# The first cell's images: copied raw from the input into the cell's own rows and normalised there, in place of a normalised tile that is stored and loaded again

## The reference

```python
for col in range(4):
    for row in range(4):
        if col == 0: ins = [input_tensor] if row == 0 else [outs[row - 1][-1]]
        elif row == 0: ins = [outs[row][0], outs[row + 1][1]]
        elif row == 3: ins = [outs[row][0], outs[row - 1][-1]]
        else: ins = [outs[row][0], outs[row + 1][1], outs[row - 1][-1]]
        outs[row] = _cell(W[col, row], b[col, row], ins)   # conv 3x3, bias, relu, split into right/up/down
return outs[-1][0]
```

## Time and profile before

| | us |
|---|---|
| median of 3 runs (lowest, highest) | 1264.2 (1263.89, 1266.4) |
| profiled execution, its own time | 1268.22 |
| its span | 1266.4 |
| PE busy | 1184.0 (93%) |
| DVE, ACT, POOL busy | 767.2, 676.1, 385.3 |
| granted TensorE clock, mean | 0.984 |

### The profile page before, as it was taken

The page is one execution under the profiler, slowest core; times in us unless marked ns, Lnnn a source line. Parts: engine busy times, 40 slices in busy tenths (PEclk is TensorE's granted clock), DMA queues, the critical chain, the costliest instruction groups (busy, mean ns, idle before and its releaser), DMA issues.

```text
span 1266.4 us, 15022 instructions
## 1 busy us (share of the span) xinstructions
PE 1184.0 (93%) x5178; PEld 878.6 (69%) x5178; DVE 767.2 (61%) x967; ACT 676.1 (53%) x737; POOL 385.3 (30%) x552
## 2 busy tenths in 40 slices
PE   2889999999999999989999999999999997999995
PEld 2656677666666677766666677777777775777773
DVE  6898962455656522245664652226665789989952
ACT  2677754344454434445444443344444789789821
POOL 7322233334512012412113213633233542104212
PEclk9999999999999999989999999999999998999997
DMA  6799998999999967899999987988789424776773
GB/s 172 225 251 251 278 270 244 180 169 205 212 199 201 228 184 205 214 177 208 200 212 185 195 224 203 246 213 224 195 210 201 58 33 73 108 114 109 125 124 59
DMA packets 103183, 233.67 MB, mean 185 GB/s; under 512 B 35316, under 2 KB 48196, under 8 KB 94724
## 3 DMA queue, kind: packets, MB, share of 16 engines
q1 hardware_dynamic: 80608, 179.28, 64.9%
q0 software_dynamic: 16064, 24.70, 10.7%
q10 hardware_dynamic: 6436, 28.74, 7.3%
HBM read 123.59 MB, written 85.19 MB: 165 GB/s over the span
## 4 chain that ended last, share of the span: by engine, by line
PE 59%; SPq 14%; DVE 12%; issue 6%; DMA 5%; ACT 3%; POOL 1%; DVEq 0%; ACTq 0%; POOLq 0%
PE PB L1736 52%; SPq L808 11%; PE PB L1705 5%; DMA F<-F 2%; DVE S L1586 2%; DVE S L1573 2%; DVE S L1579 1%; DVE F L1566 1%; SPq L839 1%; DMA S<-lattice 1%; DMA lattice<-S 1%; ACT F L1144 1%; SPq L790 1%; PE PB L1696 1%; DVE F L1449 1%
## 5 line engine op out<-in xcount | busy, mean ns | idle before, releaser
L1736 PE MATMUL PB<-F,WA 128*96 128x512 f32 (+1 forms) x3792 | 916.4, 403 | 22.2 <-DVE F L1461 9.0
L1736 PEld LDWEIGHTS PB<-F,WA 128*96 128x96 f32 (+1 forms) x3792 | 661.1, 175 | 268.5 <-ACT F L1144 16.8
L1144 ACT ACTIVATE F<-S 128x2116 fp32r<-128x2116 f32 (+4 forms) x160 | 261.5, 1635 | 212.8 <-issue 75.4
L1155 ACT ACTIVATE S<-PB,BIAS 96x512 f32<-96x512 f32 (+1 forms) x320 | 212.5, 683 | 272.2 <-PE PB L1736 270.1
L1449 DVE TENSOR_TENSOR F<-S,F 128x1089 fp32r<-128x1089 f32 (+2 forms) x80 | 121.5, 1518 | 172.4 <-ACT F L1144 171.6
L1451 DVE TENSOR_TENSOR F<-S,F 128x1058 fp32r<-128x1058 f32 x64 | 80.7, 1261 | 187.5 <-ACT F L1144 186.8
L1461 DVE CAST F<-F 64x528 fp32r<-64x528 f32 (+4 forms) x304 | 184.6, 657 | 3.5
L906 POOL DMA_DIRECT2D WA<-taps x76 | 56.9, 750 | 356.7 <-ACT S L1155 304.2
L1705 PE MATMUL PB<-F,WA 128*128 128x512 f32 x576 | 144.5, 407 | 14.9 <-DVE F L1566 14.9
L1705 PEld LDWEIGHTS PB<-F,WA 128*128 128x128 f32 x576 | 110.2, 193 | 43.6 <-issue 16.0
L1452 DVE TENSOR_TENSOR F<-S,F 64x1058 fp32r<-64x1058 f32 x64 | 82.0, 1282 | 0.0
(11 more groups left out here) (131 smaller groups left out, 742.0 us busy)
## 6 DMA issues: line engine op xcount, KB each, us to landing
S<-lattice SPq DMA_DIRECT2D x448, 66.1 KB, 5.2
lattice<-S SPq DMA_DIRECT2D x32, 817.5 KB, 6.1
S<-lattice SPq DMA_DIRECT2D x158, 136.1 KB, 3.4
S<-lattice SPq DMA_DIRECT2D x72, 272.5 KB, 5.3
lattice<-S ACTq DMA_DIRECT2D x50, 272.5 KB, 4.7
lattice<-S ACTq DMA_DIRECT2D x16, 817.5 KB, 6.6
lattice<-S SPq DMA_DIRECT2D x48, 272.5 KB, 3.9
S<-lattice SPq DMA_DIRECT2D x158, 70.1 KB, 3.2
```

Source lines behind the costliest of these rows:

```text
L1144: act.activation(piece_view(s, h, 0), raw_view(s, h), ACT.Copy).then_inc(hi_ready, 1)
L1155: act.activation(wide(to[:, at:at + TS])[:, :, 0:RX], pixels(RING_BANK[n % SLOTS_O][0:cell.rows, :]), ACT.Relu, bias=BIAS[0:cell.rows, k:k ...
L1736: last = nc.tensor.matmul(bank, WA[0:rows, first:first + cell.rows], wide(FZ[0:rows, i % SLOTS_F, base:base + TS])[:, :, 0:RX], start=j == ...
```

## The change

The tile XN, its stores, the copies between tiles and the loads of cell 0 from HBM go. In their place SP loads each image of x raw, a second time, into partitions 64 to 127 of its own slot, in four DMAs: two sets of rows, each twice, for even and odd columns (`copy_loads`). Each moves 16 channels x 32 rows of 64 floats, 128 KB. ACT (`upper_rows`) and DVE (`image_rows`) read these with a stride of two columns and write the normalised image into partitions 0 to 63 of the same slot; a masked product and two memsets on DVE put back the zeros of the border. Scale and bias are now made for 128 partitions x 8 images, since an image's rows carry the image in the free index: PE's product on the statistics has 16 columns in place of 2.

Around it: three loads of constants become one; the table of ACT is loaded early; cell 0's tap stores and loads are halved between SP and POOL; the stores of cell 0's outputs move from ACT's queue to SP's; the raw taps of cell 2 and those of two later convolutions are loaded by SP behind all images; the memsets of the start are cut to borders and spread differently over DVE and POOL. Cells 1 to 15 and all that follows are the same.

```diff
@@ layout and DMAs of an image
+        def image_copy(b):
+            at = b % SLOTS_K * PIECE
+            return flat[COPY_ROWS:P, at:at + COPY_SIZE]
+        def copy_loads(b):
+            rows = image_copy(b)
+            for r in range(2):
+                src = x[b].rearrange("c (i r) w -> r c i w", r=2)[r]
+                for s in range(2):
+                    first = r * WD + s
+                    dst = rows[r * HALO + s:(r + 1) * HALO:2, first:first + HT // 2 * WD]
+                    yield dst.rearrange("c (i w) -> c i w", w=WD), src
@@ SP
-            sp.wait_ge(turned, TURN_AT["cell0"])
-            load_taps(2)
-            sp.wait_ge(xn_act, 1)
-            sp.wait_ge(xn_dve, 1)
+            def load_copy(b):
+                if b >= SLOTS_K:
+                    sp.wait_ge(image_ready, b - SLOTS_K + 1)
+                for dst, src in copy_loads(b):
+                    sp.dma_start(dst, src).then_inc(copy_loaded[b % SLOTS_K], 16)
+            sp.wait_ge(kr_clear, 1)
+            for b in range(3):
+                load_copy(b)
...
+            for dst, src in first_half(tap_stores("cell0")):
+                sp.dma_start(dst, src).then_inc(tp0_stored, 16)
+            load_copy(3)
...
+            for dst, src in first_half(cell_spread(cells[0])):
+                sp.dma_start(dst, src).then_inc(w0_loaded, 16)
+            for b in range(HALF, B):
+                load_copy(b)
+            load_taps(2)
...
-                if ACT_STORED <= s // B < NC - 1:
+                if s < B or ACT_STORED <= s // B < NC - 1:
@@ ACT
+            def upper_rows(b):
+                rows = slice(COPY_ROWS, P)
+                act.wait_ge(copy_loaded[b % SLOTS_K], dma_total(copy_loads(b)) * (b // SLOTS_K + 1))
+                if b >= SLOTS_K:
+                    act.wait_ge(raw_read, copied_before[b - SLOTS_K + 1])
+                last = normalise(image_part(b, False), copy_part(b, False), b, rows)
+                if b % 2:
+                    last = normalise(image_part(b, True), copy_part(b, True), b, rows)
+                last.then_inc(upper_ready, 1)
...
-            for r, s, h in XN_ORDER[0::2]:
-                last = normalise(xn_rows(r, s, h), channel_rows(r, s, h), 0)
-            last.then_inc(xn_act, 1)
...
-            for i in range(2):
-                for dst, src in input_stores(i):
-                    act.dma_start(dst, src).then_inc(input_stored[i], 16)
+            upper_rows(0)
+            split_hi(0, 0)
+            upper_rows(1)
+            split_hi(1, 0)
+            upper_rows(2)
             turned_hi_part("cell1")
...
+                if s + 3 < B:
+                    upper_rows(s + 3)
@@ DVE
+            def image_rows(b):
+                rows = slice(COPY_ROWS, P)
+                if b % 2 == 0:
...
+                    nc.vector.tensor_scalar(image_part(b, True), copy_part(b, True), RS[rows, b:b + 1],
+                                            NBI[rows, b:b + 1], ALU.mult, ALU.add).then_inc(dve_step, 1)
...
+                dve.wait_ge(upper_ready, b + 1)
+                raw = raw_slot(b)
+                ends = wide(raw[0:COPY_ROWS, 0:PATCH])[:, :, 0:RW:RW - 1]
+                nc.vector.tensor_tensor(ends, ends, MASK[:, :].rearrange("p (q m) -> p q m", q=1)
+                                        .broadcast_to([COPY_ROWS, PATCH // RW, 2]), ALU.mult).then_inc(dve_step, 1)
...
+                nc.vector.memset(raw[0:HALO, TS:EVEN], 0.0)
+                nc.vector.memset(raw[HALO:COPY_ROWS, 0:RW], 0.0).then_inc(image_ready, 1)
```

More of the change, by code:

```diff
@@ L435, in piece_view, with copy_part, image_part @@
             return to.rearrange("p (t f) -> p t f", t=4) if cell.kind == "33" else to
[L437 to L444, removed]
+        def image_copy(b):
[9 more added lines that the diff above has]
+                    yield dst.rearrange("c (i w) -> c i w", w=WD), src
+        def copy_part(b, lower):
+            rows = image_copy(b)
+            if lower:
+                return rows[:, WD:WD + RQ * 2 * WD].rearrange("p (q f) -> p q f", f=2 * WD)[:, :, 0:WD + 1:2]
+            return rows.rearrange("p (q f) -> p q f", f=2 * WD)[:, :, 0:WD + 1:2]
+        def image_part(b, lower):
+            raw = raw_slot(b)[0:COPY_ROWS]
+            return wide(raw[:, EVEN:PATCH] if lower else raw[:, 0:EVEN])
         def row_halves(b, s):
             return OT[:, b % 2].rearrange("p y (w s) -> p s y w", s=2)[:, s]
-        XN_ORDER = [(r, s, h) for r in range(2) for s in range(2) for h in range(2)]
         def staged(s):
@@ L516, in output_stores @@
                 yield from image_store(k, b, st)
[L518 to L532, removed]
         def image_store(p, b, st):
@@ L794, in _ @@
                 q, before = halves_before[s] % SLOTS_K, last_user[s]
[L795 to L801, removed]
-                    for i in range(2):
-                        sp.wait_ge(input_stored[i], 2 * 16)
-                        sp.wait_ge(image_loaded[i], loads_after[i])
                 if k:
+                    if COPIES[cells[before // B].kind]:
+                        sp.wait_ge(raw_read, copied_before[before + 1])
+                    else:
+                        sp.wait_ge(lo_ready, pieces_before[before + 1])
                     sp.wait_ge(image_stored[b], 16 * stores_before[k])
-                for dst, src in direct_loads(s) if s < INPUT_PARTS[0] else input_loads(s):
-                    sp.dma_start(dst, src).then_inc(image_loaded[q], 16)
+                    for dst, src in input_loads(s):
+                        sp.dma_start(dst, src).then_inc(image_loaded[q], 16)
                 if s >= STORE_LAG:
@@ L856, in _ @@
             pool.memset(NHALF[:, :], -0.5).then_inc(pool_const, 1)
-            pool.memset(flat[:, 0:2 * PIECE], 0.0).then_inc(kr_clear, 1)
-            pool.memset(ST[:, :, :], 0.0).then_inc(st_clear, 1)
+            pool.memset(W3[:, :, :, :].bitcast(F32), 0.0).then_inc(wa_clear, 1)
+            for start in (0, SEG + 1):
+                pool.memset(ST[:, :, start:start + 1], 0.0)
+                pool.memset(ST[:, :, start + RW:start + LEAD:RW], 0.0)
+                pool.memset(ST[:, :, start + LEAD:start + TOP], 0.0)
+                pool.memset(ST[:, :, start + HOFF + RW:start + SEG:RW], 0.0)
+            last = pool.memset(ST[:, :, SEG:SEG + 1], 0.0)
+            last.then_inc(st_clear, 1)
+            pool.memset(FZ[:, :, 2 * PIECE:FSLOT].bitcast(F32), 0.0).then_inc(wa_clear, 1)
             pool.wait_ge(pool_const, 1)
@@ L990, in spread_kan @@
                     pool.dma_start(dst, src).then_inc(w2_loaded, 16)
-            store_taps("cell0")
-            norm(slice(1, 2), slice(0, 1), 1)
+            pool.wait_ge(turned_hi, TURN_AT["cell0"])
+            pool.wait_ge(turned_lo, TURN_AT["cell0"])
+            for dst, src in second_half(tap_stores("cell0")):
+                pool.dma_start(dst, src).then_inc(tp_stored, 16)
+            norm(slice(0, B), slice(0, B), 1)
+            pool.wait_ge(tp0_stored, dma_total(first_half(tap_stores("cell0"))))
+            pool.wait_ge(tp_stored, tp_after["cell0"])
+            for dst, src in second_half(cell_spread(cells[0])):
+                pool.dma_start(dst, src).then_inc(w0_spread, 16)
             clear_taps("cell1")
-            for dst, src in cell_spread(cells[0]):
-                pool.dma_start(dst, src).then_inc(w0_loaded, 16)
             store_taps("cell1")
@@ L1116, in _ @@
             act.dma_start(OB_IN[1:2, :], l3bias.rearrange("(a c) -> a c", a=1)).then_inc(bias_loaded, 16)
+            act.wait_ge(pool_const, 1)
+            act.activation(VE[:, 0:1], TWOS[:, :], ACT.Copy)
             def turned_hi_part(name):
@@ L1394, in _ @@
             dve.wait_ge(dve_step, next(steps))
[L1395 to L1402, removed]
-            dve.wait_ge(bias_loaded, 3 * 16)
-            for yi in range(YI):
-                nc.vector.tensor_copy(BN_REP[:, yi], BN_IN[:, :])
-                last = nc.vector.tensor_copy(OB_REP[:, yi], OB_IN[:, :])
@@ L1408, in _ @@
-            last.then_inc(bias_rep, 1)
-            turned_lo_part("cell1")
-            clear_weights()
+            m, v = MV[:, 1:2, 0], MV[:, 1:2, 1]
+            nc.vector.tensor_tensor(NV[:, 1:2], m, m, ALU.mult).then_inc(dve_step, 1)
+            dve.wait_ge(dve_step, next(steps))
+            nc.vector.scalar_tensor_tensor(v, v, GN_EPS, NV[:, 1:2], ALU.add, ALU.add).then_inc(dve_step, 1)
+            dve.wait_ge(dve_step, next(steps))
+            nc.vector.tensor_tensor(MV_OWN[:, :, :], MV[:, 1:2, :].broadcast_to([P, B, 2]),
+                                    OWN.rearrange("p (b a) -> p b a", a=1).broadcast_to([P, B, 2]), ALU.mult)\
+                .then_inc(mv_ready, 1)
```

119 lines of the change are left out of this document (71 added, 48 removed).

## The result

Slower, where 1260.2 us was forecast: 1270.15 us median (1265.23 to 1278.94, 17 runs) against 1264.2 us of the kernel before on the same chip (17 runs, one of them at 1440.89 us, far from all others). The ratio is 1.0041, 95% interval 1.0025 to 1.0057, about 5.2 us more; it is an estimate from the single runs and not the quotient of the two medians, which would be 1.0047. The time lies outside the range of 1254 to 1269. The profiled execution took 1278.94 us, 8.8 above its median, so its trace holds more loss than a usual execution; I read mainly the first 80 us of it and take sizes from ratios.

The account below looks back on a forecast made before the run. Cells 1 and 2 were taken as DMA-bound, PE as the bound from 160 us. DMA work 4.5 us further on at 60 us cuts PE's waits by about 4: median 1264.2 becomes 1260.2 us, range 1254 to 1269.

Parts of the forecast that it names:

- the ledger: DMA work to 60 us: 24.6 us added, 14.1 removed, net +10.5, leaving DMA work 4.5 us further on.
- the stuck taps: Slower rival, chance 0.23: cell 2's raw taps wait in SP's queue behind image 7; 1272 us at 36.6 ns a piece.
- An image at 3.07 us: DMA cost of loading one raw image: 2048 pieces of 256 B at 24 ns over 16 engines, ends 2.1 and 4.7.
- the slower rival's 29: Price in ns of a 256 B piece from which the slower rival, chance 0.23, decides (3.7 us an image).
- Scale and bias at 15: Before cell 0: scale and bias ready at 15 us, 1 us earlier than before.
- Cell 0 at 28: Cell 0's first matmul at 28 us, 5 us earlier, decided by the landing of the tap loads.
- Turn's wait 2 to 3 us, end 41.6: PE's turn of cell 2's taps, inside cell 0: new wait for raw taps, ending about 41.6 instead of 44.9.
- End of cell 0 at 57.8 to 60: PE's end of cell 0, against 59.4 before: the 5 us head start becomes 0 to 1.6.
- the 38.4 of the sum: Time in us when raw images 4 to 7 drain from SP's queue: 26.1 + 4c, c being one image's DMA cost.
- 15 of 18 free microseconds: DMA time free in the first 60 us: 18 us, of which 3 stay free and 15 can be filled.
- PE's waits should shrink by 4: Cells 1 and 2: PE's 8.9 us of waits shrink by about 4 through a shorter DMA backlog.
- Kept to the end: From 160 us PE is the bound, so a time shift reaching 160 us should be kept to the end.

Follow-up runs that it names:

- e6: Kernel before with only cell 0's output stores moved from ACT's to SP's queue: 1276.01 us, ratio 1.0068 to the kernel before.
- e10: Same edit as e6 to the kernel before, on another chip: 1277.30 us, ratio 1.0092 to the kernel before.
- e5: The changed kernel run again as it is, with a second trace: 1271.12 us, ratio 1.0033 to the kernel before.
- e1: Changed kernel with cell 0's output stores back in ACT's queue: 1264.45 us, ratio 0.9982 to the kernel before.
- e4: Changed kernel reading raw images as 8 KB runs, same bytes, another arrangement of rows: 1268.88 us, ratio 1.0015 to the kernel before.
- e3: Changed kernel with cell 0's stores back in ACT's queue and cell 2's raw taps loaded earlier: 1263.84 us, ratio 0.9971 to the kernel before.
- e11: Kernel before plus sixteen small unneeded DMAs in SP's queue, without waits for ACT's evacuation: 1272.39 us, ratio 1.0045 to the kernel before.
- e9: Kernel before, stores still in ACT's queue, plus sixteen small unneeded DMAs in SP's queue behind the moved stores' waits: 1276.41 us, ratio 1.0091.

## Why the prediction was wrong

The step that failed is one sentence of the ledger: "The moved stores (16 issues of about 0.55 us, ACT to SP) change nothing here, since SP has no loads for cell 0 left to issue." The size of the issues was nearly right (1.23 us for two, 0.62 each). The reason was about the wrong cell: behind the stores in SP's queue stand the thirty loads of cell 1, and these took SP 5.3 us an image before, against PE's 4.98, so nothing was free. I read the free time of the DMA engines and not that of the queue that starts them. e6 puts the price at 8.6 us (5.5 to 11.8 by its interval), e10 at 11.6; within the changed kernel, it is 1.0041 (e5: 1.0033) against e1's 0.9982, about 7.5 us (6.5), each ratio from another chip. It is no rival either: the slower one, the stuck taps, had another place.

Point by point:
- An image at 3.07 us: too low. SP issued the last four in 12.09 us, 3.02 each, but they landed more slowly: the first load of image 4 at 28.2 (issued at 25.09, landed 3.1 later), the last of image 7 at 41.2 (36.31 and 4.9), 3.5 us an image. Over the stretch from 9 to 28 us a packet took 29.7 ns (102.4% of 16 x 19 us over 10493), in place of 24, with the engines full. That is the slower rival's 29, but with its stuck taps the turn should have come behind 44, and it came at 41.6. e4, with large pieces, is not told from the kernel before (1.0015) and its first stall in cell 1 is the same: the pieces are not the main cause.

```profile
q1 hardware_dynamic: 10493, 2.70, 102.4%
```

- The Trainium skill's line that transfers under 512 B fall short of line rate ("DMA: Bandwidth & Descriptors", Specifications): the trace agrees, 256 B in 29.7 ns is 8.6 GB/s an engine, where the tile's larger packets ran at 17.4. It pointed at a true cost that was not the one that mattered most.
- Scale and bias at 15: wrong, 17.5. POOL now takes the power for all eight images in one instruction of 1.67 us, begun at 15.53. It cost nothing that the trace shows, since the weights decided, as forecast:

```profile
15.53 1.67 POOL L904 TENSOR_TENSOR RS<-VE,NHALF 128x8 f32<-128x8 f32 x1 [0.82 <-DVE VE L1404]
```

- Cell 0 at 28: 27.06, waiting for the tap load. Turn's wait 2 to 3 us, end 41.6: 3.31 and 42.4. End of cell 0 at 57.8 to 60: 59.4. These held, with two errors of opposite sign in them, which is luck: the images drained later than the 38.4 of the sum (the last one landed at 41.2), and cell 0 started almost 1 us ahead of it.
- The ledger: 15 of 18 free microseconds filled. The share reached 1.02, so that part came. PE's waits should shrink by 4 and grew, by 5.6 in the first trace and by 1.6 in e5's. With the stores back in ACT's queue they shrink: 5.6 us in e1's trace for 8.9. e1's ratio gives 2.3 us of gain for the rest of the change (a loss of 0.5 to a gain of 5.1), and e5 less e6 gives about 4.4: about the forecast 4, not well told from none.
- "Kept to the end": the changed kernel's loss is about what its first 160 us show; of e3's lead only a part was kept.

## What to carry to other kernels

When an instruction moves to another engine's queue, list what stands behind it there until the next point at which that queue is idle, for the next stage too, not only for the one being changed. Compare what the queue takes for one unit of work, waits and slow issues included, with the bound engine's time for it: here it was 5.3 us against 5.0 already, and 6.0 with two stores in it. Look first at what stands ahead of the next stage's first load. A share of the DMA engines under one does not say that there is room in the queue that feeds them.

## What the runs showed of the hardware

- SP's time for an issue hardly depends on the bytes: 0.71 us for a load from the lattice (six in 4.28), 0.62 for a store of 272.5 KB, 0.52 to 0.58 for 3 KB. These are quiet stretches; the same six loads took up to 6.77 us (the row at 72.26 after).
- The Trainium skill says that queues of different engines end on the same 16 engines ("DMA: Bandwidth & Descriptors", Issuing engines are not separate DMA queues), and that spreading issues saves only the time to initiate a DMA, "usually small relative to the DMA itself". One load's 0.71 us is small beside its landing, 3.4 to 5.9 us behind its issue in the changed kernel; but landings overlap and issues in one queue don't, and here the issue time alone cost 5.7 us (e11).
- A stretch with 215 GB/s in place of 238 is by itself no sign of a slower queue: it came with the stores' bytes in another queue too (e9).
- After 5.12 us without work PE was granted half its clock (0.50, 1.2 GHz) from 67.9 to 72 us (e6); without that wait it kept 1.00 from 63.2 to 78 (e1).
- The same edit cost 0.68% on one chip and 0.92% on another (e6, e10), within both intervals.
